# Decay stage: the products of q and k with their tables, on VectorE straight from PSUM

## The chip, the cores and the metric

One Trainium2 chip, one core of it. The kernel is one program on that core; the metric is the device time in microseconds (us), median of the runs shown. Engines are named as in the profile: PE (TensorE matrix products), PEld (its weight loads), DVE (VectorE), ACT (ScalarE), POOL (GpSimd), SP (SyncE).

## The reference, cut to what matters

Six blocks follow each other: two convolution blocks, an attention, a mixture of experts, a second attention ("L3", with a decay instead of a softmax) and a last mixture. The change lies in L3. For each of 16 images of 1024 tokens, taken as 4 sequences of 256 in blocks of 8 heads of 16 numbers:

```python
q = (x @ wq_w.T + wq_b).reshape(b, l, h, d)
k = (x @ wk_w.T + wk_b).reshape(b, l, h, d)
v = (x @ wv_w.T + wv_b).reshape(b, l, h, d)
phase = phazor_p / jnp.abs(phazor_p)
amp = jax.nn.sigmoid(amplitude)
phazor = phase * amp[:, None]
...
qc = q.astype(cplx) * (phazor_prog * phazor[None])[None]
cross = jnp.einsum('blhd,hde->blhe', qc, last_conv)
mask = jnp.where(tril[None], amp[:, None, None] ** jnp.where(tril, diff, 0)[None], 0.0)
qph = q.astype(cplx) * phase_prog[None]
kph = k.astype(cplx) * phase_prog_inv[None]
...
inner = jnp.einsum('bhlm,bmhd->blhd', qk_mask, v.astype(cplx))
out = (inner + cross).real.astype(x.dtype).reshape(b, l, h * d)
```

Each of q and k, bias added, is thus multiplied by tables over position and channel: k by one (`tab_k`), q by two (`tab_k` for the scores, `tab_s` for the state that comes from earlier chunks).

## The kernel before

The stages run one after the other; `decay_stage` (L2320) handles L3. It loops over 16 images (`images`, L2496: images -1, 0, 1, 14, 15, 16 written out, 2 to 13 in a loop). An image is 4 items (a = 0 to 3), an item being one half of the image's 1024 tokens (a // 2) and one group of 4 heads (a % 2); an item has 4 chunks of 128 tokens (c = 0 to 3). Item number w is 4 n + a. Every engine walks the same 16 places (a, c) of an image in an order written out by hand (`slots`, L2496 ff.), and they keep each other in step by counting semaphores. There is no scheduler.

At each place, in this order:

- PE (`body`, L3106): at c = 0 it projects the keys of the *next* item into `ps_q`, at c = 1 the queries of the next item (`project`, L3033); at c = 0 the scores of this item (`score`, L3051: 16 products of 32 rows into `ps_s`); in items 1 and 3 the keys and values in token order (`mix`, L3041); then transposes into `ps_x`, and `chunk` (L3063): the product with the state (`ps_o`), the new state (`ps_st`), and after c = 1 and c = 3 the inner products (L3093).
- DVE (`body`, L2877): at c = 0 `masked` for chunks 0 and 1 (scores times decay, `d_inner`, L2777), then one `masked` at each of c = 1 and c = 2; in items 1 and 3 `end_keys` (`d_k_tok`, `d_v_tok`, L2785); at c = 1 `add_item` (L2802); `new_state` (L2793), for which PE waits at the next chunk; in item 0 `combine` (L2865, L2867) and layer-norm statistics; in item 3 the gates.
- ACT (`body`, L2952): `copy_projection` (L2946) at c = 0 and 1, which adds the bias and writes `raw` in SBUF; the normalisations, the copies of `ps_x` and of `ps_o` (`d_o_chan`).
- POOL (`body`, L2625): in items 1 to 3, at each c, it waits until `masked` of this chunk is done and issues 1 or 2 of the 16 gathers of image n + 2 (`gather`, L2556, an indirect DMA of 128 rows; `GATHERS_AT`, L2447); at c = 0, behind them, `with_tables` (L2610): three products from `raw` with the tables. The gathers of c = 1 to 3 are queued behind these three.

`ps_q` is one buffer for both projections: PE's next `project` waits on `p_copied`, ACT's on `tables_used`.

Of the kernel before, what the change touches and what calls it, by code (L numbers as in the profile page):

```python
# [9 lines left out]
ALU = mybir.AluOpType  # L10
ACT = mybir.ActivationFunctionType
AX = mybir.AxisListType

P = 128
# [6 lines left out]
HALF = 512  # L21
# [2287 lines left out]
CHUNKS = 4  # L2309
# [10 lines left out]
def decay_stage(nc, T, route, slots_out, xT_dram, gates, ident, dram):  # L2320
    with ExitStack() as ctx:
        sb, ps, sem = allocator(nc, ctx)
# [12 lines left out]
        row = sb("d_row", [P, 2, 5])  # L2335
# [27 lines left out]
        tab_k = sb("d_tab_k", [P, 2, P])  # L2363
# [14 lines left out]
        shift = [sb(f"d_shift{k}", [P, TILES]) for k in range(2)]  # L2378
        xn = [sb(f"d_xn{k}", [P, PX]) for k in range(2)]
        xT = [sb(f"d_xT{k}", [P, PX]) for k in range(2)]  # L2380
        raw = sb("d_raw", [P, 2, HALF])
        q_chan = sb("d_q_chan", [P, 2, HALF])
        q_state = sb("d_q_state", [P, 2, HALF])
        k_chan = sb("d_k_chan", [P, 2, HALF])
# [39 lines left out]
        x_ready = sem("d_x_ready")  # L2424
        x_free = sem("d_x_free")
        p_ready = sem("d_p_ready")
        p_copied = sem("d_p_copied")
        tables_used = sem("d_tables_used")
        k_ready = sem("d_k_ready")
        k_done = sem("d_k_done")  # L2430
# [20 lines left out]
        def positive(eng, s, value):  # L2451
            if not (isinstance(value, int) and value <= 0):
                eng.wait_ge(s, value)
# [92 lines left out]
        def _(pool):  # L2546
# [60 lines left out]
                pool.wait_ge(rstd_done[k], 4 * m + 3)  # L2607
                nc.gpsimd.tensor_tensor(shift[k][:], zero[:], shift[k][:], ALU.subtract).then_inc(rstd_done[k], 1)  # L2608

            def with_tables(w, g, k):  # L2610

                pool.wait_ge(p_copied, 2 * w + 1)
                positive(pool, chunk_done, 4 * (w - 1))
                nc.gpsimd.tensor_tensor(
                    k_chan[:, k].rearrange("p (c l) -> p c l", c=CHUNKS),
                    raw[:, 0].rearrange("p (c l) -> p c l", c=CHUNKS),
                    tab_k[:, g:g + 1].broadcast_to([P, CHUNKS, P]), ALU.mult).then_inc(tables_used, 1)
                pool.wait_ge(p_copied, 2 * w + 2)
                for out, table in ((q_chan, tab_k), (q_state, tab_s)):
                    nc.gpsimd.tensor_tensor(  # L2620
                        out[:, k].rearrange("p (c l) -> p c l", c=CHUNKS),
                        raw[:, 1].rearrange("p (c l) -> p c l", c=CHUNKS),
                        table[:, g:g + 1].broadcast_to([P, CHUNKS, P]), ALU.mult).then_inc(tables_used, 1)

            def body(n):  # L2625
                finish, prepare, _ = parts_of(n)
                if isinstance(n, int) and n < 0:
                    scales(0, 0)
                for a, c, steps, nxt in slots(n):
                    if a and gathers(n):  # L2630
                        first = sum(some for at, some in GATHERS_AT.items() if at < (a, c))
                        if steps:
                            wait_apart(pool, inner_done, 4 * (4 * n + a) + c + 1, passed)
                        gather(n + 2, first, first + GATHERS_AT[a, c])
                    if (a, c) == (0, 3) and finish:
                        scales(n - 1, 1)
                    if (a, c) == (1, 3) and prepare and not (isinstance(n, int) and n < 0):
                        scales(n + 1, 0)
                    if c == 0 and nxt:
                        with_tables(4 * n + a + 1, (a + 1) % 2, (a + 1) % 2)  # L2640

            pool.wait_ge(step, TABLE_STEPS)
            images(pool, body)
# [2 lines left out]
        def _(dve):  # L2646
# [125 lines left out]
            def masked(w, c, g):  # L2772
# [4 lines left out]
                tt(inner[:, c].rearrange("p (j l) -> p j l", j=GH), ps_s[:, :, c * P:(c + 1) * P],  # L2777
                   decay[:, g * GH:(g + 1) * GH], ALU.mult).then_inc(inner_done, 1)

            def end_keys(n, half, c):  # L2780

                at = 8 * n + 4 * half + c
                dve.wait_ge(k_ready, at + 1)
                positive(dve, chunk_done, 4 * (4 * (n - 1) + 2 * half + 2))
                tt(k_tok[:, half, c], ps_k[:, 0:2 * P], tab_end[:].rearrange("p g r -> p (g r)"), ALU.mult)  # L2785
                nc.vector.tensor_copy(v_tok[:, half, c, :, 0:DH],
                                      ps_k[:, 2 * P:3 * P].rearrange("p (h e) -> p h e", h=HD)).then_inc(k_done, 1)
# [89 lines left out]
            def body(n):  # L2877
# [5 lines left out]
                    statistics(0, 0, 1)  # L2883
                for a, c, steps, nxt in slots(n):
                    w = 4 * n + a
                    if steps and c == 0:
                        masked(w, 0, a % 2)
                    if steps and c < CHUNKS - 1:
# [28 lines left out]
        def _(act):  # L2917
# [25 lines left out]
                    positive(act, xT_sent, 16 * (n - 1))  # L2943
                nc.scalar.activation(xT[k][:, half * HALF:half * HALF + HALF], ps_x[:], ACT.Copy).then_inc(x_free, 1)

            def copy_projection(w, g, kind):  # L2946
                act.wait_ge(p_ready, 2 * w + kind + 1)
                positive(act, tables_used, 3 * (w - 1) + (3 if kind else 1))
                nc.scalar.activation(raw[:, kind], ps_q[:], ACT.Identity, bias=row[:, g, 4 - kind:5 - kind]
                                     ).then_inc(p_copied, 1)  # L2950

            def body(n):  # L2952
                finish, prepare, _ = parts_of(n)
                first = isinstance(n, int) and n < 0
# [2 lines left out]
                    normalise(0, 0, 1)  # L2957
                for a, c, steps, nxt in slots(n):
                    w = 4 * n + a
                    if nxt and c < 2:  # L2960
                        copy_projection(w + 1, (a + 1) % 2, c)
                    for name in filled_at(n, a, c):
                        if name != "logits":
                            read_out(n, name)
# [15 lines left out]
        def _(pe):  # L2980
# [52 lines left out]
            def project(w, a, kind):  # L3033

                g, half = a % 2, a // 2
                positive(pe, p_copied, 2 * w + kind)
                weights = wq[:, g] if kind else wkv[:, g * P:(g + 1) * P]
                mm(ps_q[:], weights, xT[0][:, half * HALF:half * HALF + HALF], start=True, stop=True
                   ).then_inc(p_ready, 1)
# [166 lines left out]
```

## Time and profile before

| | |
|---|---|
| median of 3 runs | 4375.7 us (4369.7 to 4379.16) |
| the profiled execution | span 4435.5 us |
| decay stage in it | from about 2650 us to 3680 us; images 1 to 13 take 754 us |
| PE / DVE / ACT / POOL busy, whole span | 83% / 71% / 49% / 44% |

The page gives the busy time of each engine, the span in 40 slices, and the groups of instructions by line. The time of the profiled execution is known only by its span, and 59.8 us (1.4%) above the median of the runs that were not profiled. The queries used here are the windows (busy time of each engine in a stretch, with the granted TensorE clock), the groups by line, the waits, single lines, and the instructions in order of time.

### The profile page before, as it was taken

Reading aid. Unit: us, or ns where it says so; the run is one execution under the profiler, and the core shown is the slowest. Engines: PE = TensorE matmul, PEld = TensorE weight load, DVE = VectorE, ACT = ScalarE, POOL = GpSimd, SP = SyncE. Lnnn points to the kernel's source line nnn. Section 1 sums busy time; section 2 is a strip of 40 time slices with the busy share of each in tenths; the row PEclk is TensorE's granted clock in tenths of the full one; section 3 lists DMA queues with packets and bytes.
Section 4 is the critical chain, followed back from the end, with each engine's and each line's share of the span. In section 5 each row is a group of like instructions: output and inputs, shape, how many; then the busy total and the mean of one; then the engine's idle time right before and its main releaser. Section 6 shows DMA issues by size and latency. Waiting matters only on the chain. (4 is left out here: it accounts for less than half of the span.)

```text
span 4435.5 us, 74474 instructions
## 1 busy us (share of the span) xinstructions
PE 3699.2 (83%) x21807; PEld 1993.2 (45%) x21809; DVE 3136.1 (71%) x6481; ACT 2174.3 (49%) x3800; POOL 1933.4 (44%) x2119
## 2 busy tenths in 40 slices
PE   2479999999999999999569962888888886999999
PEld 0212333333333333332258851555555555777777
DVE  7478888888887878887156646555555557877777
ACT  3326666666666666666357740222222223444443
POOL 1111333233223333332345552666666644777776
PEclk9679999999999999999789985999999998999999
DMA  2121111122222222220033320000000001000000
GB/s 97 20 37 28 31 30 30 30 38 38 36 37 38 38 39 38 38 37 11 18 117 103 103 78 10 25 29 28 26 28 28 27 16 34 24 24 24 24 20 23
DMA packets 98451, 166.17 MB, mean 37 GB/s; under 512 B 27904, under 2 KB 33288, under 8 KB 98072
## 3 DMA queue, kind: packets, MB, share of 16 engines
q1 hardware_dynamic: 81208, 129.14, 12.2%
q0 software_dynamic: 16384, 33.59, 2.7%
q8 instruction: 134, 2.20, 0.2%
q14 instruction: 149, 1.22, 0.1%
q10 hardware_dynamic: 576, 0.02, 0.0%
HBM read 89.70 MB, written 72.97 MB: 37 GB/s over the span
## 5 line engine op out<-in xcount | busy, mean ns | idle before, releaser
L1214 ACT ACTIVATE b_probs<-b_ps_s 128x512 f32<-128x512 f32 x2048 | 1174.4, 596 | 673.0 <-PE b_ps_s L1258 609.9
L1016 DVE TENSOR_REDUCE b_maxes<-b_ps_m 128x1 f32<-128x1024 f32 x1024 | 1218.2, 1216 | 312.9 <-PE b_ps_m L1246 288.4
L1258 PE MATMUL b_ps_s<-b_qs,b_ks 99*128 99x512 bf16 x2048 | 790.6, 390 | 83.8 <-DMA b_qs<-b_m_parts 23.4
L1246 PE MATMUL b_ps_m<-b_ks,b_qs 96*128 96x512 bf16 x2048 | 638.5, 394 | 64.2 <-DVE b_maxes L1016 43.5
L1985 POOL TENSOR_TENSOR e_act_lo<-e_act,e_act_hi 128x512 fp32r<-128x512 f32 x384 | 522.6, 1361 | 238.9 <-DVE e_act_hi L1914 238.9
L1258 PEld LDWEIGHTS b_ps_s<-b_qs,b_ks 99*128 99x128 bf16 x2048 | 198.7, 98 | 882.5 <-ACT b_probs L1214 668.2
L1270 PE MATMUL b_ps_o<-b_probs,b_vs 128*32 128x512 f32 x4096 | 551.8, 611 | 23.6 <-ACT b_probs L1214 22.8
L2186 ACT ACTIVATE e_act<-e_ps_h,e_bias 128x512 f32<-128x512 f32 x384 | 264.4, 689 | 411.3 <-PE e_ps_h L2240 290.6
L935 POOL DMA_INDIRECT slots_in<-b_xn,b_slot x256 | 251.6, 983 | 413.2 <-ACT b_probs L1214 367.0
L2089 DVE TENSOR_TENSOR e_act<-e_act,e_ps_g 128x512 f32<-128x512 f32 x384 | 261.6, 682 | 145.7 <-ACT e_act L2186 145.7
L2777 DVE TENSOR_TENSOR d_inner<-d_ps_s,d_decay 128x512 f32<-128x512 f32 x256 | 169.3, 682 | 221.6 <-PE d_ps_s L3059 109.3
L2556 POOL DMA_INDIRECT d_y<-slots_out,d_slot_now x256 | 248.5, 971 | 121.1 <-issue 59.0
L1246 PEld LDWEIGHTS b_ps_m<-b_ks,b_qs 96*128 96x128 bf16 x2048 | 193.0, 100 | 236.8 <-DVE b_maxes L1016 107.3
L1914 DVE CAST e_act_hi<-e_act 128x512 fp32r<-128x512 f32 x384 | 244.6, 637 | 0.0
L2238 PE MATMUL e_ps_h<-e_x_hi,e_w_hi 128*128 128x512 f32 x384 | 159.0, 414 | 47.8 <-DVE e_x_lo L2073 42.5
L2971 ACT ACTIVATE d_o_chan<-d_ps_o 128x512 f32<-128x512 f32 x64 | 38.2, 597 | 322.4 <-PE d_ps_o L3093 283.3
L1577 DVE SCALAR_TENSOR_TENSOR c_act<-c_ps_h,c_bias,c_half_way 128x512 f32<-128x512 f32 x142 | 106.5, 750 | 101.5 <-ACT c_half_way L1658 98.9
L2934 ACT ACTIVATE d_xn<-tokens,d_shift,d_rstd 128x128 f32 (+1 forms) x256 | 104.9, 482 | 138.4 <-POOL d_shift L2608 138.4
L1270 PEld LDWEIGHTS b_ps_o<-b_probs,b_vs 128*32 128x32 f32 x4096 | 81.2, 108 | 197.3 <-issue 143.3
L897 POOL TENSOR_TENSOR b_taken<-b_hit 128x64 bf16<-128x64 f32 x16 | 5.2, 323 | 361.0 <-DVE b_hit L1077 361.0
L2250 PE MATMUL e_ps_y<-e_act_hi,e_w_hi 128*128 128x512 f32 x384 | 152.4, 397 | 1.1 <-POOL e_act_lo L1985 1.1
L2239 PE MATMUL e_ps_h<-e_x_lo,e_w_hi 128*128 128x512 f32 x384 | 153.1, 399 | 0.0
(462 smaller groups left out, 7089.7 us busy)
## 6 DMA issues: line engine op xcount, KB each, us to landing
b_qs<-b_q_parts SPq DMA_DIRECT2D x96, 256.0 KB
c_xin<-slots_in SPq DMA_DIRECT2D x71, 256.0 KB, 2.6
slots_out<-c_y_out SPq DMA_DIRECT2D x71, 256.0 KB, 2.0
b_q_parts<-b_qparts SPq DMA_DIRECT2D x16, 768.0 KB
a_x<-in_x_dram SPq DMA_DIRECT2D x8, 1024.0 KB, 10.2
normalised_t<-d_xT SPq DMA_DIRECT2D x16, 512.0 KB
e_xb<-normalised_t SPq DMA_DIRECT2D x32, 256.0 KB, 2.8
out_dram<-e_total SPq DMA_DIRECT2D x32, 256.0 KB, 2.0
```

Source lines behind the costliest of these rows:

```text
L935: nc.gpsimd.indirect_dma_start(out=slots_in, out_offset=bass.IndirectOffsetOnAxis(ap=slot[:, i:i + 1], axis=0), in_=xn[1][:, j * P:(j + 1) ...
L1016: nc.vector.tensor_reduce(maxes[:, kv, u:u + 1], ps_m[:, u % 2], AX.X, ALU.max).then_inc(m_free, 1)
L1214: nc.scalar.activation(probs[:, s % PROBS, j * HALF:(j + 1) * HALF], ps_s[:, j % 2], ACT.Exp).then_inc(exp_done, 1)
L1246: last = nc.tensor.matmul(ps_m[:, u % 2, half * HALF:(half + 1) * HALF], qs[0:STACK, buffer, h * PX + qt * P:h * PX + qt * P + P], ks[0:ST ...
L1258: nc.tensor.matmul(ps_s[:, j % 2], ks[0:rows, parity, kv * PX + tt * P:kv * PX + tt * P + P], qs[0:rows, parity, h * PX + half * HALF:h * ...
L1270: last = nc.tensor.matmul(ps_o[32 * j:32 * j + 32, :], vs[:, parity, tt, g // 2, :], probs[:, s % PROBS, j * HALF:(j + 1) * HALF], start=( ...
L1914: copy(act_hi[:, u % ring_a], act_buf[:, u % RING]).then_inc(hi_done, 1)
L1985: nc.gpsimd.tensor_tensor(act_lo[:, u % ring_a], act_buf[:, u % RING], act_hi[:, u % ring_a], ALU.subtract).then_inc(lo_done, 1)
L2089: nc.vector.tensor_tensor(act_buf[:, u % RING], act_buf[:, u % RING], ps_g[:, (u // units_of_gate) % 2], ALU.mult).then_inc(weighed, 1)
L2186: nc.scalar.activation(act_buf[:, u % RING], ps_h[:, u % ring_h, 0], ACT.Gelu, bias=bias[:, bias_column(u, 0)]).then_inc(a_ready, 1)
L2556: nc.gpsimd.indirect_dma_start(out=y[:, i // TILES, i % TILES], out_offset=None, in_=slots_out, in_offset=bass.IndirectOffsetOnAxis(ap=slo ...
L2777: tt(inner[:, c].rearrange("p (j l) -> p j l", j=GH), ps_s[:, :, c * P:(c + 1) * P], decay[:, g * GH:(g + 1) * GH], ALU.mult).then_inc(inn ...
```

## The change

VectorE computes (ps_q + bias) * table in one `scalar_tensor_tensor` from PSUM, three times an item, each into the same tile as before. ACT's copy, POOL's three products, the tile `raw` and the semaphore `p_copied` are gone. PE's `project` now waits for VectorE's reads of `ps_q` (`tables_used`).

```diff
@@ POOL
-            def with_tables(w, g, k):
-                pool.wait_ge(p_copied, 2 * w + 1)
-                positive(pool, chunk_done, 4 * (w - 1))
-                nc.gpsimd.tensor_tensor(k_chan[:, k]..., raw[:, 0]...,
-                    tab_k[:, g:g + 1].broadcast_to([P, CHUNKS, P]), ALU.mult).then_inc(tables_used, 1)
-                pool.wait_ge(p_copied, 2 * w + 2)
-                for out, table in ((q_chan, tab_k), (q_state, tab_s)):
-                    nc.gpsimd.tensor_tensor(out[:, k]..., raw[:, 1]..., table..., ALU.mult).then_inc(tables_used, 1)
...
-                    if c == 0 and nxt:
-                        with_tables(4 * n + a + 1, (a + 1) % 2, (a + 1) % 2)
@@ DVE
+            def keys_with_table(w, g):
+                dve.wait_ge(p_ready, 2 * w + 1)
+                positive(dve, chunk_done, 4 * (w - 1))
+                stt(laid(k_chan[:, g]), laid(ps_q[:]), row[:, g, 4:5], tab_k[:, g:g + 1].broadcast_to([P, CHUNKS, P]),
+                    ALU.add, ALU.mult).then_inc(tables_used, 1)
+
+            def queries_with_tables(w, g):
+                dve.wait_ge(p_ready, 2 * w + 2)
+                for out, table in ((q_chan, tab_k), (q_state, tab_s)):
+                    stt(laid(out[:, g]), laid(ps_q[:]), row[:, g, 3:4], table[:, g:g + 1].broadcast_to([P, CHUNKS, P]),
+                        ALU.add, ALU.mult).then_inc(tables_used, 1)
...
                 for a, c, steps, nxt in slots(n):
                     w = 4 * n + a
+                    if nxt and c == 0:
+                        keys_with_table(w + 1, (a + 1) % 2)
+                    if nxt and c == 1:
+                        queries_with_tables(w + 1, (a + 1) % 2)
                     if steps and c == 0:
                         masked(w, 0, a % 2)
@@ ACT
-                    if nxt and c < 2:
-                        copy_projection(w + 1, (a + 1) % 2, c)
@@ PE, project
-                positive(pe, p_copied, 2 * w + kind)
+                positive(pe, tables_used, 3 * w + kind)
```

PE's order is the same in both. DVE's order in item 3 (shown of image 14, which is written out), from the start of the item to the keys in token order of chunk 1 (`d_k_tok`, for which PE waits), before (L2777 is `masked`, L2785 `end_keys`, L2793 `new_state`, L2809 to L2819 the gates):

```order
L2777 TENSOR_TENSOR d_inner<-d_ps_s,d_decay 128x512 x2
L2785 TENSOR_TENSOR d_k_tok<-d_ps_k,d_tab_end 128x256
L2786 COPY d_v_tok<-d_ps_k 128x8x16
L2793 TENSOR_TENSOR d_state<-d_ps_k,d_block_mask 128x128
L2809 TENSOR_TENSOR d_logits<-d_ps_x,d_bg 128x64
L2816 MAX d_top<-d_logits 128x8 x8
L2819 TENSOR_TENSOR d_gap<-d_top 128x8
L2777 TENSOR_TENSOR d_inner<-d_ps_s,d_decay 128x512
L2785 TENSOR_TENSOR d_k_tok<-d_ps_k,d_tab_end 128x256
```

and in the change (its lines are numbered anew: L2768 and L2775 are the new products, L2758 `masked`, L2783 `end_keys`, L2791 `new_state`):

```order
L2768 SCALAR_TENSOR_TENSOR d_k_chan<-d_ps_q,d_row,d_tab_k 128x512
L2758 TENSOR_TENSOR d_inner<-d_ps_s,d_decay 128x512 x2
L2783 TENSOR_TENSOR d_k_tok<-d_ps_k,d_tab_end 128x256
L2784 COPY d_v_tok<-d_ps_k 128x8x16
L2791 TENSOR_TENSOR d_state<-d_ps_k,d_block_mask 128x128
L2807 TENSOR_TENSOR d_logits<-d_ps_x,d_bg 128x64
L2814 MAX d_top<-d_logits 128x8 x8
L2817 TENSOR_TENSOR d_gap<-d_top 128x8
L2775 SCALAR_TENSOR_TENSOR d_q_chan<-d_ps_q,d_row,d_tab_k 128x512
L2775 SCALAR_TENSOR_TENSOR d_q_state<-d_ps_q,d_row,d_tab_s 128x512
L2758 TENSOR_TENSOR d_inner<-d_ps_s,d_decay 128x512
L2783 TENSOR_TENSOR d_k_tok<-d_ps_k,d_tab_end 128x256
```

One product now stands ahead of the first `masked`, and two ahead of that of chunk 2 and of everything of chunk 1 behind it.

POOL's order from item 1 into item 2 of an image (image 1, written out; L2556 is one gather), before:

```order
L2556 DMA d_y<-slots_out,d_slot_now 128x128
L2614 TENSOR_TENSOR d_k_chan<-d_raw,d_tab_k 128x512
L2620 TENSOR_TENSOR d_q_chan<-d_raw,d_tab_k 128x512
L2620 TENSOR_TENSOR d_q_state<-d_raw,d_tab_s 128x512
L2556 DMA d_y<-slots_out,d_slot_now 128x128 x5
```

and in the change, the same place in the loop (REGISTER_ALU computes the value of a wait; L2554 is one gather):

```order
L2554 DMA d_y<-slots_out,d_slot_now 128x128
L63 REGISTER_ALU
L2554 DMA d_y<-slots_out,d_slot_now 128x128
L63 REGISTER_ALU
L2554 DMA d_y<-slots_out,d_slot_now 128x128 x2
L63 REGISTER_ALU
L2554 DMA d_y<-slots_out,d_slot_now 128x128
```

The three products between the gathers are gone; each gather now stands behind its own wait (for `masked` of its chunk) alone.

## Rows read from the trace of the kernel before

**Rows 1.** Windows: length, busy time (count) by engine, granted clock, DMA share.
```profile
core 0: us, PE busy (x) PEld busy (x) DVE busy (x) ACT busy (x) POOL busy (x), PEclk, DMA share, GB/s
2794.85:3548.56 753.71, 617.54 (x5604) 414.34 (x5600) 421.88 (x1694) 212.53 (x428) 463.66 (x495) 0.92 0.09 27
3201.82:3220.02 18.20, 15.06 (x125) 9.83 (x121) 9.26 (x51) 2.18 (x4) 11.62 (x12) 0.91 0.10 29
3247.26:3257.81 10.55, 9.13 (x104) 6.40 (x101) 3.69 (x8) 6.02 (x13) 9.18 (x11) 1.00 0.20 68
3569.30:3580.48 11.18, 8.88 (x101) 5.89 (x97) 8.02 (x23) 1.97 (x3) 3.86 (x3) 0.92 0.01 2
3580.48:3596.70 16.22, 12.99 (x121) 8.63 (x117) 11.42 (x52) 6.24 (x13) 8.28 (x11) 1.00 0.01 4
3596.70:3605.38 8.68, 8.51 (x105) 6.07 (x101) 3.69 (x8) 6.24 (x13) 3.80 (x3) 1.00 0.15 58
3605.38:3620.25 14.87, 12.98 (x124) 9.01 (x121) 9.20 (x51) 2.07 (x4) 3.77 (x3) 1.00 0.01 2
...
3220.02:3230.92 10.90, 8.49 (x101) 5.93 (x97) 8.75 (x28) 1.86 (x3) 3.89 (x3) 0.95 0.02 6
3230.92:3247.26 16.34, 14.12 (x120) 8.91 (x116) 11.08 (x50) 6.24 (x13) 10.93 (x14) 0.93 0.06 16
```

**Rows 2.** Waits of PE and DVE in 2700:3560: total us, times, longest.
```profile
PE d_ps_k L3084 <- DVE d_v_tok L2786: 53.0, 51, 4.4
...
DVE d_inner L2777 <- remote: 109.0, 15, 8.1
```

**Rows 3.** Groups by line, 3000:3600: shapes, count, busy us, mean ns, idle before.
```profile
L2777 DVE TENSOR_TENSOR d_inner<-d_ps_s,d_decay 128x512 f32<-128x512 f32 x166 | 109.7, 682 | 147.6 <-remote 79.7 <-PE d_ps_s L3059 67.9
...
L2614 POOL TENSOR_TENSOR d_k_chan<-d_raw,d_tab_k 128x512 f32<-128x512 f32 x42 | 53.8, 1281 | 47.9 <-ACT d_raw L2949 47.1
```

**Rows 4.** Single lines: duration in ns as minimum/median/maximum.
```profile
L1577 DVE SCALAR_TENSOR_TENSOR c_act<-c_ps_h,c_bias,c_half_way x142: 735/751/752, 2260.0 to 2620.4; 128x512 f32<-128x512 f32 x142
...
L2865 DVE SCALAR_TENSOR_TENSOR d_y<-d_y,d_weight_now,tokens x128: 337/344/2327, 2725.1 to 3577.8; 128x128 f32<-128x128 f32 x128
```

**Rows 5.** In time, item 0: start, duration, operation, idle before and releaser.
```profile
3225.99 2.14 DVE L2865 SCALAR_TENSOR_TENSOR d_y<-d_y,d_weight_now,tokens 128x128 f32<-128x128 f32 x4
3226.09 1.38 POOL L2620 TENSOR_TENSOR d_q_state<-d_raw,d_tab_s 128x512 f32<-128x512 f32 x1
...
3228.99 0.49 PE L3077 MATMUL d_ps_o<-d_q_state,d_state 128*128 128x128 f32 x2 [1.92 <-DVE d_state L2793]
```

**Rows 6.** In order of time, chunk 1 of item 3, image 14.
```profile
3613.80 0.46 PE L3084 MATMUL d_ps_k<-d_state,d_turn 128*128 128x128 f32 x2 [0.40 <-DVE d_v_tok L2786]
```

**Rows 7.** In order of time, chunk 1 of item 2 in a late image.
```profile
3600.69 0.69 ACT L2949 ACTIVATE d_raw<-d_ps_q,d_row 128x512 f32<-128x512 f32 x1 [0.61 <-PE d_ps_q L3038]
...
3601.12 0.42 DVE L2802 TENSOR_TENSOR tokens<-tokens,d_ps_x 128x256 f32<-128x256 f32 x1
...
3602.26 0.66 PE L3027 MATMUL d_ps_x<-ident,d_xn 128*128 128x128 f32 x4
```

**Rows 8.** In time, start of item 3: image with gathers, then one without.
```profile
3204.79 0.95 POOL L2556 DMA_INDIRECT d_y<-slots_out,d_slot_now  x1 [0.30 <-issue]
...
3206.94 1.29 DVE L2777 TENSOR_TENSOR d_inner<-d_ps_s,d_decay 128x512 f32<-128x512 f32 x2 [8.05 <-remote]
...
3208.81 0.49 PE L3084 MATMUL d_ps_k<-d_state,d_turn 128*128 128x128 f32 x2 [1.40 <-DVE d_v_tok L2786]
...
3607.67 1.29 DVE L2777 TENSOR_TENSOR d_inner<-d_ps_s,d_decay 128x512 f32<-128x512 f32 x2 [3.75 <-PE d_ps_s L3059]
...
3610.45 0.39 PE L3084 MATMUL d_ps_k<-d_state,d_turn 128*128 128x128 f32 x2
```

**Rows 9.** In order of time, item 0 of the first image.
```profile
2758.20 0.95 POOL L2556 DMA_INDIRECT d_y<-slots_out,d_slot_now  x1 [0.30 <-issue]
...
2760.70 3.11 DVE L2865 SCALAR_TENSOR_TENSOR d_y<-d_y,d_weight_now,tokens 128x128 f32<-128x128 f32 x4 [4.90 <-DMA d_y<-slots_out,d_slot_now]
```

More of the change, by code:

```diff
@@ L2380, in decay_stage @@
         xT = [sb(f"d_xT{k}", [P, PX]) for k in range(2)]
-        raw = sb("d_raw", [P, 2, HALF])
         q_chan = sb("d_q_chan", [P, 2, HALF])
@@ L2426, in decay_stage @@
         p_ready = sem("d_p_ready")
-        p_copied = sem("d_p_copied")
         tables_used = sem("d_tables_used")
@@ L2608, in scales @@
                 nc.gpsimd.tensor_tensor(shift[k][:], zero[:], shift[k][:], ALU.subtract).then_inc(rstd_done[k], 1)
-            def with_tables(w, g, k):
-                pool.wait_ge(p_copied, 2 * w + 1)
-                positive(pool, chunk_done, 4 * (w - 1))
-                nc.gpsimd.tensor_tensor(
-                    k_chan[:, k].rearrange("p (c l) -> p c l", c=CHUNKS),
-                    raw[:, 0].rearrange("p (c l) -> p c l", c=CHUNKS),
-                    tab_k[:, g:g + 1].broadcast_to([P, CHUNKS, P]), ALU.mult).then_inc(tables_used, 1)
-                pool.wait_ge(p_copied, 2 * w + 2)
-                for out, table in ((q_chan, tab_k), (q_state, tab_s)):
[L2620 to L2623, printed above, removed]
             def body(n):
@@ L2778, in masked, with laid @@
                    decay[:, g * GH:(g + 1) * GH], ALU.mult).then_inc(inner_done, 1)
+            def laid(x):
+                return x.rearrange("p (c l) -> p c l", c=CHUNKS)
+            def keys_with_table(w, g):
[8 more added lines that the diff above has]
+                        ALU.add, ALU.mult).then_inc(tables_used, 1)
             def end_keys(n, half, c):
@@ L2944, in read_out @@
                 nc.scalar.activation(xT[k][:, half * HALF:half * HALF + HALF], ps_x[:], ACT.Copy).then_inc(x_free, 1)
[L2946 to L2950, printed above, removed]
             def body(n):
```

## The prediction, made before the changed kernel ran

> **What bounds the kernel now.** I read the windows by item first. An item runs from one key projection on PE to the next; images 1 to 13 take 753.71 us, 57.98 each, with PE busy 617.54 of it and a mean granted clock of 0.92 [rows 1]. Image 14 is the same program without gathers and shows what the bare chain takes: items 0 to 3 in 11.18, 16.22, 8.68 and 14.87 us, 50.95 together [rows 1]. Against that stand, in an image with gathers, 10.90, 16.34, 10.55 and 18.20 [rows 1]. So items 0 and 1 are as short as they can be, item 2 loses 1.9, and item 3 loses 3.3 in this image. The shown image takes 55.99; the mean one loses 7.03 (57.98 − 50.95).
>
> Then the waits: DVE stands in front of `masked` at the start of item 3 fifteen times, 109.0 us in all, and the profile names no engine for it ("remote") [rows 2]; PE waits 53.0 us in 51 places for the tokens' keys of DVE (`d_v_tok`) [rows 2]. In order of time at item 3: the item starts at 3201.82 [rows 1]; POOL's last gather runs from 3204.79 for 0.95 us; DVE's `masked`, which waits for PE's score products, starts at 3206.94 after 8.05 us idle, 5.12 after the item's start; PE's chunk product stands until 3208.81, 1.40 of it for DVE [rows 8]. In the image without gathers the same `masked` starts 2.29 after the item's start (3607.67 − 3605.38) and the chunk product 5.07 after (3610.45 − 3605.38), not 6.99 [rows 1, 8]. The hold is thus 2.8 us on DVE and about 1.9 to 2.0 on PE, and it ends 1.2 us after the last gather's end. I read it so: the completion of PE's narrow score products is seen late while POOL's gathers are in flight. Why these gathers lie there: POOL works in order, and the gathers of places 1 to 3 are queued behind three table products of 1281 ns each [rows 3], which wait for both projections. They come out in a burst at the end of the item and fall on the scores of the next one.
>
> So in this stage PE and DVE hand work to each other, and PE is late where DVE is late; POOL and ACT are not the bound but POOL decides when gathers go.
>
> **The change part by part.** Every time below is for one image (4 items) unless said.
>
> *Removed from ACT:* eight copies of PSUM, 0.69 us each [rows 7], with ACT busy 2.2 of 18.2 us in item 3 and 6.0 of 10.6 in item 2 [rows 1]. No wait of PE rests on them; in item 2 ACT's other copies feed PE and move 0.7 earlier, but DVE is later there (below). Worth 0.
>
> *Removed from POOL:* twelve products of 1.28, 15.4 us of the 35.7 it is busy (463.66 / 13) [rows 1, 3]. By itself nothing waits for that; it moves the gathers, priced below.
>
> *Added to DVE:* twelve `scalar_tensor_tensor` of 128x512, one input in PSUM. The nearest row is the same operation on the same shape out of PSUM with a second tensor in SBUF, 735 to 752 ns, median 751 [rows 4]; the lower bound is the product without the bias, 682 [rows 3]. I take 0.75: 9.0 us an image, on a DVE that is busy 32.5 of 58 (421.88 / 13) [rows 1]. What of it lies on the path:
>
> - Item 0. At its start DVE has the key product extra, while its first `masked` waits for PE anyway; 0.7 of idle covers it. The two query products (1.5) come at chunk 1, ahead of `masked` and `new_state`, for which PE already waits 1.92 us [rows 5]. No cover: +1.4 with 0.1 of overlap. Against it stands a gain. DVE's four combine steps took 2.14 us there while a POOL product ran beside them for 1.38 [rows 5]; their usual length is 0.337, their longest 2.327 [rows 4]. Four undisturbed take 1.35, and with no POOL product beside them they give back the 2.14 − 1.35 = 0.8, and 1.0 where one takes 1.36. I take 1.0. Sum +0.4.
> - Item 1. The same 1.4 at chunk 1, and at chunk 0 DVE is still at the statistics of the layer norm when the keys come, (it is busy 11.08 of 16.34 there [rows 1]), so that I estimate half of a key product (0.4) to delay `masked`. +1.8.
> - Item 2. PE does not wait for DVE in chunk 1, but DVE's addition to `tokens` (3601.12, 0.42 long) must precede PE's transposes at 3602.26: slack 0.7 [rows 7]. The queries are there at 3600.69, when ACT takes them [rows 7], and with 1.5 of products ahead of `masked` and of the addition, the addition moves by up to 1.6. 1.6 − 0.7 = +0.9.
> - Item 3. At chunk 1 PE waits 0.40 for `d_v_tok` [rows 6], so the queries' 1.4 goes through. At chunk 0 DVE idles 3.75 us even without gathers [rows 8], which hides the key product. +1.4.
>
> Together +4.5 on DVE's part of the chain; with 0.682 for a product +3.9; and with nothing covered 9.0 − 1.0 = +8.0.
>
> *Gained by moved gathers.* The change puts each gather behind its own `masked` alone. They then spread over the item, and no burst should fall on the next scores: item 2 gets back 10.55 − 8.68 = 1.9, item 3 its 2.0 [rows 1, 8]. −3.9, between −3.9 and 0. In the first image a combine takes 3.11 us after 4.90 of waiting for a gather's data; its gather ran at 2758.20 [rows 9]. There the next images' gathers come about 3.7 us (three products) earlier. −4 once.
>
> *The rest of the loss.* 7.03 − 3.9 = 3.1 us an image is neither bare chain nor hold. The granted clock is 0.91, 0.95, 0.93 and 1.00 in items 3, 0, 1 and 2 with gathers, and 0.92, 1.00, 1.00, 1.00 without [rows 1]; the two levels are 2.4 and 1.2 GHz, and the low one follows PE's idle time, that in front of `d_v_tok` in item 3 foremost. With the holds gone, that idle time (1.40) is gone, but PE idles 1.4 longer at each chunk 1. It lies between 0 (as in image 14) and 3.1 (as now). I take 1.1, nearer the row without holds.
>
> An image is then 50.95 + 4.5 + 1.1 = 56.5, against 57.98: −1.5, and −19.5 for thirteen. Image 14 has no hold to lose: +4.5, and +1.0 for some low clock, +5.5. The last has no next projection after its third item: +3. The first: −4. Sum −15. The profiled execution, 4435.5, would be 4420.5. Its 59.8 above the median is a length of the whole program under the profiler and I leave it in place: 4375.7 − 15 = **4361**.
>
> *New waits.* PE's next `project` waits for DVE's last read of `ps_q`. That read comes within 3 us of the projection and the next one is over 5 us off: nothing. DVE waits for `p_ready` with `masked`, `d_k_tok` and `new_state` queued behind. PE projects first in each place, so this wait is for one product, 0.6 to 0.7 us, and is in the terms above.
>
> **The rivals.**
>
> *A. The holds stay* (slower). The gathers still run on POOL, still 16 an image; if the late completion comes from something else at the start of items 2 and 3, or the spread gathers hit other narrow products (the inner ones after chunks 1 and 3), then nothing of the 3.9 comes back. It decides as soon as less than 2.5 us an image is regained with the clock as forecast (4.5 − 2.0), less than 4.5 with the clock as now. At nothing regained an image is 50.95 + 4.5 + 3.9 + 3.1 = 62.5: 13 × 4.5 = +58, then +5.5, +3 and −4 for image 14, the last and the first: 4438. For it: the profile gives no releaser for DVE's wait ("remote"), only coincidence in time. Against it: the 2.29 and 5.12 us of [rows 8], and items 0 and 1, over which no burst falls and which are not longer than in image 14 [rows 1]. A page bears on this rival, and by it the time would be that of A. The Trainium skill, page "SBUF — State Buffer", section "SBUF: two separate sides", says that engines' and DMAs' ports do not contend and that only VectorE and GpSimd share a pair, while PE never waits for anyone; by that rule gathers could not hold PE's products. The same section has that a shared pair is locked for a whole instruction; by that rule, the combine of [rows 5] stands still for POOL's product, and the trace agrees (2.14 for 1.35). Chance 0.2.
>
> *B. The holds go, but the clock loss stays as now,* 3.1 an image in place of 1.1, since PE idles 1.4 longer four times. 13 × (−1.5 + 2.0) = +6.5, image 14 +7, the ends −1: +12, 4388. For it: the clock fell in items 0, 1 and 3, behind idle times of 1 to 2 us. Against it: image 14 ran at 1.00 through items 1 to 3 with waits of 0.4 for DVE [rows 1, 6]. Chance 0.25, of which a third ends within 0.2%.
>
> *C. More is gained:* clock as in image 14, a product at 0.68: 13 × (−1.5 − 1.1 − 0.6) = −42, image 14 +4, the ends −1: −39, and with half of the 0.6 −35: some 4338. Chance 0.1.
>
> *D. The scores come no earlier for DVE but the burst only moves* into items 0 or 1, with half of the hold left. +25 against the forecast: 4386, the same as B. It is in B's chance.
>
> **How the numbers follow.** The forecast (0.45) is 4361 with 4345 to 4377 from its own terms (half a microsecond an image on the clock, as much on the DVE terms). A 0.2, B with D 0.25, C 0.1. A measurement of this kernel tells about 0.2%, 8.7 us, from no change. Faster: most of the forecast (0.36) and C (0.10), 0.46. Within 0.2%: 0.09 of the forecast, 0.08 of B, 0.04 of A where part is regained: 0.21. Slower: 0.16 of A, 0.17 of B: 0.33. The range 4335 to 4420 holds the forecast, C nearly whole and B; out of it stay A with nothing regained, and little below.
>
> **What would show each step.** The new products read 0.68 to 0.75 each. DVE's "remote" wait ahead of `masked` in item 3 is gone, and `masked` starts 2.3 us after the item; if it still starts 5 us after, A. The windows give item 2 at about 9.6, item 3 at 16.3 to 17; item 0 at 11.5 and item 1 at 18. The longest step of L2865 (now L2863) falls from 2.3 to under 1 us. PE's waits for `d_v_tok` and `d_state` at chunk 1 grow by 1.4 each; a growth of more than 2 makes the DVE terms too small. The clock of images 1 to 13 rises above 0.95 for the forecast, stays at 0.92 for B. In image 14, which has no gathers, the DVE terms stand alone: 50.95 should become 55.5 to 56.5.

## The result, and the profile after

The change makes the kernel slower: 4399.16 us (4394.34 to 4401.94, 4 runs) against 4374.86 (4369.7 to 4379.16, 4 runs), a ratio of 1.0056 with a 95% interval of 1.0042 to 1.0071. That is +24 us where −15 was forecast: inside the stated range, on the other side of zero, in the place of rival B (4388). But it did not come about as B said.

The first thing to see is a contradiction. The profiled execution of the changed kernel has a span of 4397.3 us, 2 below its own time; that of before, on which every term of the prediction rests, 4435.5, 60 above the times of before. By the two profiles the change gains 38 us, by the timed runs it loses 24. So the kernel before was profiled once more (first run below). From here on "before" is that second execution, span 4366.7, and where the first is meant the text says so.

Windows of before (second execution): twelve images from one start of item 3 to another (2842.05 to 3485.89), then items 3, 0, 1 and 2 of one image. Columns as in [rows 1]:

```profile
core 0: us, PE busy (x) PEld busy (x) DVE busy (x) ACT busy (x) POOL busy (x), PEclk, DMA share, GB/s
2842.05:3485.89 643.84, 536.42 (x5189) 364.95 (x5185) 389.58 (x1596) 197.76 (x396) 426.79 (x457) 0.96 0.10 29
3379.28:3394.05 14.77, 13.04 (x124) 9.02 (x120) 9.14 (x51) 2.13 (x4) 11.26 (x12) 1.00 0.12 31
3394.05:3404.51 10.46, 8.06 (x101) 5.71 (x97) 8.18 (x24) 1.97 (x3) 4.65 (x4) 0.99 0.04 13
3404.51:3421.33 16.82, 14.60 (x120) 9.40 (x117) 11.51 (x52) 6.24 (x13) 10.97 (x14) 0.90 0.05 16
3421.33:3431.87 10.54, 8.67 (x104) 6.07 (x100) 3.69 (x8) 6.12 (x13) 9.18 (x11) 0.99 0.21 68
```

The same of the changed kernel, the twelve images and one image with gathers:

```profile
2844.82:3507.75 662.93, 536.77 (x5189) 365.64 (x5185) 472.94 (x1740) 135.15 (x300) 243.11 (x313) 0.96 0.09 29
3118.91:3134.99 16.08, 13.04 (x124) 9.02 (x120) 11.20 (x54) 0.81 (x2) 5.01 (x6) 1.00 0.09 25
3134.99:3146.86 11.87, 9.17 (x101) 6.54 (x97) 10.36 (x32) 0.60 (x1) 0.00 (x0) 0.89 0.00 0
3146.86:3163.74 16.88, 13.45 (x121) 8.82 (x117) 12.16 (x50) 4.98 (x11) 10.70 (x16) 0.98 0.08 23
3163.74:3173.66 9.92, 8.60 (x105) 6.08 (x101) 5.66 (x11) 4.86 (x11) 4.52 (x5) 1.00 0.22 79
```

An image of before takes 53.65 us (643.84 / 12), not the 57.98 of [rows 1]; one of the changed kernel 55.24. PE's own work is the same to 0.1% (536.42 and 536.77) at the same clock, so what was added is waiting. DVE works 83 us more, 7 an image; POOL 184 less, ACT 63 less. Item 3, which in [rows 1] took 18.20, takes 14.77 in the image shown, no more than in the image without gathers (14.87). Over the twelve images it averages 15.4 (184.68 / 12): seven times 14.8 to 14.9, five times 15.8 to 16.5 with a granted clock of 0.89 to 0.93. Item 2 loses most, 10.54 here and 11.1 on average (133.07 / 12) against 8.68; the changed kernel has 9.92 there, and 9.93 on average.

The last image but one has no gathers, so none has a part in how the two kernels differ there. Its items 0 to 3 in the changed kernel, to hold against the rows from 3569.30 on in [rows 1]:

```profile
3523.83:3535.31 11.48, 8.88 (x100) 6.25 (x97) 10.07 (x31) 0.60 (x1) 0.00 (x0) 0.91 0.01 1
3535.31:3552.60 17.29, 13.70 (x120) 8.83 (x117) 12.50 (x51) 4.97 (x11) 4.52 (x8) 0.96 0.01 3
3552.60:3562.11 9.51, 8.55 (x104) 6.07 (x100) 5.66 (x11) 4.86 (x11) 0.00 (x0) 1.00 0.13 52
3562.11:3578.30 16.19, 12.98 (x124) 9.02 (x120) 11.25 (x54) 0.81 (x2) 0.00 (x0) 1.00 0.01 2
```

Single lines of the changed kernel, the answers to [rows 3] and [rows 4] (duration in ns as minimum/median/maximum): the three new products and the combine.

```profile
L2768 DVE SCALAR_TENSOR_TENSOR d_k_chan<-d_ps_q,d_row,d_tab_k x64: 717/750/753, 2741.7 to 3604.5; 128x512 f32<-128x512 f32 x64
...
L2775 DVE SCALAR_TENSOR_TENSOR d_q_chan<-d_ps_q,d_row,d_tab_k x64: 731/750/752, 2745.0 to 3607.4; 128x512 f32<-128x512 f32 x64
L2775 DVE SCALAR_TENSOR_TENSOR d_q_state<-d_ps_q,d_row,d_tab_s x64: 739/742/748, 2745.7 to 3608.0; 128x512 f32<-128x512 f32 x64
...
L2863 DVE SCALAR_TENSOR_TENSOR d_y<-d_y,d_weight_now,tokens x128: 337/343/353, 2724.5 to 3531.8; 128x128 f32<-128x128 f32 x128
```

The products cost what the nearest row said, and no combine step is stretched any more.

### The profile page after: what moved, and what is told of

It is laid out like the page before. It is cut to its first block and busy times, and to the rows that moved or that the text cites. A ratio compares the mean times of both kernels' runs of the same rounds, so it can differ in the third digit from the quotient of the medians.

```text
span 4397.3 us, 74090 instructions
## 1 busy us (share of the span) xinstructions
PE 3660.1 (83%) x21809; PEld 1973.2 (45%) x21809; DVE 3241.9 (74%) x6673; ACT 2091.6 (48%) x3672; POOL 1685.1 (38%) x1927
## 5 line engine op out<-in xcount | busy, mean ns | idle before, releaser
L2554 POOL DMA_INDIRECT d_y<-slots_out,d_slot_now x256 | 245.1, 957 | 261.6 <-DVE d_inner L2758 181.6
L2758 DVE TENSOR_TENSOR d_inner<-d_ps_s,d_decay 128x512 f32<-128x512 f32 x256 | 169.2, 682 | 20.9 <-PE d_ps_s L3053 20.9
L2230 PE MATMUL e_ps_g<-e_g_rows,e_spread 128*128 128x512 f32 x384 | 150.9, 393 | 2.3 <-DVE e_act L2089 2.3
```

Of the source, the lines that this page charges most:

```text
L2554: nc.gpsimd.indirect_dma_start(out=y[:, i // TILES, i % TILES], out_offset=None, in_=slots_out, in_offset=bass.IndirectOffsetOnAxis(ap=slo ...
```

## The experiments

### The kernel before, profiled again

No edit.

> The kernel before once more, to see how its profiled execution stands to its timed runs. Theory 1: the late products at the start of items 2 and 3 (PE's scores seen late while gathers run) belong to that one profiled execution and not to the runs that were timed; a second profile then has a span near 4374 us, images of 53 to 54.5 us in the middle, and DVE's waits for 'remote' in item 3 are few. Theory 2: they come with every profile of this kernel and not in timed runs: span again 4430 to 4440, images of 58. Theory 3: they are in the timed runs too, and the 60 us are elsewhere: span between the two, images of 58. Ratio 1.000 in all.

Measured: 4370.24 us against 4371.46 for the copies of before beside it (ratio 0.9997, 0.9986 to 1.0009), profiled span 4366.7. Of 34 timed runs of before in these experiments none was above 4384.7. Theory 1 holds: the images take 53.65 us, and no wait of DVE is put down to "remote". The start of an item 3 in this execution, in order of time (start, duration, operation, idle before and what ended it), to hold against [rows 8]:

```profile
3378.86 1.00 POOL L2556 DMA_INDIRECT d_y<-slots_out,d_slot_now  x1 [0.16 <-issue]
...
3380.17 0.95 POOL L2556 DMA_INDIRECT d_y<-slots_out,d_slot_now  x1 [0.30 <-issue]
3380.34 0.98 PEld L3059 LDWEIGHTS d_ps_s<-d_q_chan,d_k_chan 32*128 32x128 f32 x32 [0.76 <-issue]
3380.34 1.17 PE L3059 MATMUL d_ps_s<-d_q_chan,d_k_chan 32*128 32x128 f32 x32
...
3381.42 0.95 POOL L2556 DMA_INDIRECT d_y<-slots_out,d_slot_now  x1 [0.30 <-issue]
...
3381.68 1.29 DVE L2777 TENSOR_TENSOR d_inner<-d_ps_s,d_decay 128x512 f32<-128x512 f32 x2 [4.45 <-PE d_ps_s L3059]
```

Gathers run before, beside and after the scores, as in the first execution, and yet `masked` starts 0.17 us after the scores end (3380.34 + 1.17), with PE and not "remote" as releaser. That is 2.40 after the item's start at 3379.28, as without gathers (2.29). The first execution has the hold in fourteen items 3, with 2.5 to 3.7 us from the end of the scores to `masked` (and once in an item 2); in the same fourteen items of this one it is 0.18 us at most. The hold belonged to one of the two executions, and gathers beside the scores do not by themselves bring it about.

### The scales moved ahead on POOL

The kernel before, with one move:

```diff
                 for a, c, steps, nxt in slots(n):
+                    if (a, c) == (1, 2) and prepare and not (isinstance(n, int) and n < 0):
+                        scales(n + 1, 0)
                     if a and gathers(n):
...
-                    if (a, c) == (1, 3) and prepare and not (isinstance(n, int) and n < 0):
-                        scales(n + 1, 0)
```

> The kernel before with one move on POOL: the four small steps that make the layer-norm scales of the next image (d_rstd, d_shift) stand ahead of the gathers of item 1, chunk 2, in place of behind those of chunk 3. Theory 1 (before's item 2 takes 10.5 to 11.2 us and not 8.7 because POOL comes to these steps some 5.6 us after DVE's d_mv, its queue being filled by table products and gathers, and ACT's xn and PE's transposes wait for them): item 2 falls to 8.7 to 9.3, 1 to 2 us an image: 4345 to 4358. Theory 2 (it is the gathers themselves that hold item 2): same as before within 4 us, 4367 to 4375.

Measured: 4349.88 against 4373.2 (ratio 0.9945, 0.9925 to 0.9965), 23 us faster. Theory 1. Item 2 falls to 8.90, in eleven of twelve images, with table products and gathers all still on POOL (item 3 gives 0.6 of it back on average, so that an image takes 52.26 for 53.65):

```profile
3350.57:3359.47 8.90, 8.52 (x104) 6.06 (x100) 3.69 (x8) 6.20 (x13) 7.48 (x8) 1.00 0.26 88
```

What held item 2 is thus a chain over POOL that the prediction had not seen. In before, in order of time, from DVE's means over POOL's scales and ACT's normalisation to PE's transposes (the second set, in the item 2 that starts at 3421.33 and takes 10.54):

```profile
3415.36 0.64 DVE L2769 BATCH_NORM_AGGREGATE d_mv<-d_stats 128x2 f32<-128x6 f32 x8
...
3422.85 0.22 POOL L2602 TENSOR_TENSOR d_rstd<-d_mv,d_eps 128x8 f32<-128x8 f32 x1
...
3425.51 1.65 ACT L2934 ACTIVATE d_xn<-tokens,d_shift,d_rstd 128x128 f32 x4 [2.24 <-POOL d_shift L2608]
...
3427.63 1.64 ACT L2934 ACTIVATE d_xn<-tokens,d_shift,d_rstd 128x128 f32 x4
...
3429.88 0.65 PE L3027 MATMUL d_ps_x<-ident,d_xn 128*128 128x128 f32 x4 [1.34 <-ACT d_xT L2944]
```

The means are there at 3416.00; POOL, with two table products and four gathers still ahead, begins the scales 6.85 later. Item 2 grows with this delay: in the twelve images of before it is 5.6 to 8.7 us late, and item 2 takes 9.27 at the one end and 13.55 at the other. In `scales_early` and in the changed kernel the same two steps:

```profile
3344.60 0.64 DVE L2769 BATCH_NORM_AGGREGATE d_mv<-d_stats 128x2 f32<-128x6 f32 x8
...
3347.14 0.21 POOL L2602 TENSOR_TENSOR d_rstd<-d_mv,d_eps 128x8 f32<-128x8 f32 x1
```

```profile
3157.77 0.64 DVE L2750 BATCH_NORM_AGGREGATE d_mv<-d_stats 128x2 f32<-128x6 f32 x8
...
3160.75 0.21 POOL L2600 TENSOR_TENSOR d_rstd<-d_mv,d_eps 128x8 f32<-128x8 f32 x1
```

1.90 and 2.34 us: this is the relief that the change brings, and a move of one call brings it without loading DVE.

### Only the keys, only the queries

`keys_only` leaves `keys_with_table` on DVE and gives the queries back to ACT's copy and two POOL products; `queries_only` is the other half. Each has a semaphore of its own for keys and queries in place of `tables_used`.

```diff
 (keys_only)
                     if nxt and c == 0:
                         keys_with_table(w + 1, (a + 1) % 2)
-                    if nxt and c == 1:
-                        queries_with_tables(w + 1, (a + 1) % 2)
```

> Only the key product on DVE, straight from PSUM, at chunk 0; the queries go over ACT's copy and two POOL products as before (one POOL product fewer in front of the gathers). Theory: the key product hides under DVE's wait for the scores except in item 1: 4374 to 4382. Rival (the cost lies in the key product ahead of masked at chunk 0): 4390 or more.

> Only the two query products on DVE at chunk 1; the keys go over ACT's copy and one POOL product as before. Theory: this part carries nearly the whole of the loss: 4390 to 4400. Rival (keys carry it): 4370 to 4380.

Measured: keys only 4346.11 (ratio 0.9955, 0.9938 to 0.9972), 25 us faster than before; queries only 4395.77 (1.0056, 1.0037 to 1.0076), 24 slower. Over the twelve images:

```profile
2836.01:3460.51 624.50, 531.84 (x5188) 363.17 (x5184) 425.70 (x1644) 165.05 (x348) 366.43 (x408) 0.96 0.10 30
```

```profile
2844.60:3502.10 657.50, 527.14 (x5188) 361.88 (x5184) 438.28 (x1692) 167.95 (x348) 306.67 (x361) 0.97 0.10 29
```

52.04 and 54.79 an image. The queries carry the whole loss, as expected. The keys were expected to cost 3 to 10 us and gave 25: the key product hides under DVE's wait for the scores, and one POOL product fewer in front of the scales is a gain that no theory had named before the run. The two halves do not add up (−25 and +24 give +24 together): the relief of POOL pays once, and `queries_only` has already taken it (its item 2 averages 9.93 us, as in the full change).

> keys_only with the same move of the scales on POOL. Theory 1: keys_only took its gain (25 us) from the shorter POOL queue ahead of the scales, item 2 at 9.3; what is left there is 0.3 to 0.6 us an image: 4336 to 4346. Theory 2 (its gain comes from elsewhere): gains add up, 4325 to 4332.

Measured: 4340.83 (0.9925, 0.9902 to 0.9947). Theory 1, with its number: moving the scales gives 23 us alone and 5 to 7 on top of `keys_only` (by the medians, and by each against its own copies of before). It is in the main one and the same gain.

### One more product at chunk 1

```diff
-                for out, table in ((q_chan, tab_k), (q_state, tab_s)):
+                for out, table in ((q_chan, tab_k), (spare, tab_s), (q_state, tab_s)):
```

> The change with one more product of the queries on DVE at chunk 1 (a spare 128x512 product from PSUM into a tile that nobody reads, between the two). It prices DVE's time at that place. Theory 1 (DVE's products at chunk 1 lie on the path in items 0, 1 and 3 nearly whole, in item 2 nearly whole too): 0.75 us each, 2 to 3 us an image, 32 to 48 over the change: 4430 to 4447. Theory 2 (they are mostly covered, and the change's loss is clock or a wait of PE): below 4410.

Measured: 4447.29 (ratio to before 1.0160, 1.0137 to 1.0184), 48 over the change, the upper end of theory 1, with an image at 58.65 (703.80 / 12). The products are 64 times 0.742 = 47 us, so DVE's time at chunk 1 seems to count in full. Not all of it is waiting, though: over the twelve images (40.9 us longer, 48 products more) PE's busy time for the same matmuls grows by 15.3, from 536.77 to 552.02, at a clock of 0.93 for 0.96. That leaves 25.6 us of waiting, 0.53 for a product of 0.742; the low clock makes up the rest.

### Where DVE's products stand

Placements of the same two query products. `q_behind_state`: after `new_state` of chunk 1; `q_split`: one ahead of chunk 1, one ahead of chunk 2; `q_at_c2`: both at the end of chunk 2; `mix`: keys on DVE, queries on DVE behind `new_state` in item 2 only, else on POOL.

```diff
 (q_behind_state)
-                    if nxt and c == 1:
-                        queries_with_tables(w + 1, (a + 1) % 2)
...
                     if steps and state_index(0, a, c) is not None:
                         new_state(n, a, c)
+                    if nxt and c == 1:
+                        queries_with_tables(w + 1, (a + 1) % 2)
```

> The change with the two query products moved behind new_state in chunk 1, everything else as in the change. Theory: the cost of the change is DVE's 1.4 us ahead of masked, the tokens' keys and new_state in chunk 1, of which PE waits; with the products behind them nearly all of 1.5 us an image (24 us) comes back: 4365 to 4380. Rival (the cost comes from the moved gathers or from PE's new wait on DVE's reads of ps_q): stays within 5 us of the change, 4394 to 4404.

Measured: 4434.39 (1.0149, 1.0132 to 1.0166), 35 slower than the change: a clear miss, and neither theory had it. Item 2 did fall to 8.9. In item 3, which starts at 3130.12 here and at 3118.91 in the changed kernel, the wait moved from chunk 1 to chunk 2. The changed kernel:

```profile
3128.58 0.49 PE L3078 MATMUL d_ps_k<-d_state,d_turn 128*128 128x128 f32 x2 [1.65 <-DVE d_v_tok L2784]
...
3132.10 0.49 PE L3078 MATMUL d_ps_k<-d_state,d_turn 128*128 128x128 f32 x2 [1.01 <-DVE d_v_tok L2784]
...
3133.20 0.91 PE L3042 MATMUL d_ps_k<-d_wkv,d_xT 128*128 128x384 f32 x2 [0.38 <-DVE d_state L2791]
```

and `q_behind_state`:

```profile
3138.45 0.49 PE L3078 MATMUL d_ps_k<-d_state,d_turn 128*128 128x128 f32 x2 [0.32 <-DVE d_v_tok L2784]
...
3143.29 0.80 PE L3078 MATMUL d_ps_k<-d_state,d_turn 128*128 128x128 f32 x2 [2.32 <-DVE d_v_tok L2784]
...
3144.90 1.65 PE L3042 MATMUL d_ps_k<-d_wkv,d_xT 128*128 128x384 f32 x2 [0.38 <-DVE d_state L2791]
```

Both wait 2.65 us in two pieces and reach the product of chunk 2 equally late (13.19 and 13.17 after the item's start). But after the single wait of 2.32 the same PE work takes 1.65 in place of 0.91: the clock has gone to its low level, and the item ends at 18.12, not 16.08. Nine of the twelve items 3 of `q_behind_state` take 18.1 us. So do two of the twelve of the changed kernel, and there the clock fell behind the wait of 1.65:

```profile
3228.39:3246.52 18.13, 15.70 (x124) 10.52 (x120) 11.36 (x54) 0.81 (x2) 5.01 (x6) 0.81 0.08 22
```

One long wait thus goes with the low clock far more often than two shorter ones, but it is neither needed for it nor proven to be its cause. What the low clock costs, PE's busy time over the twelve images of `q_behind_state` shows:

```profile
2846.27:3536.28 690.01, 560.95 (x5188) 379.84 (x5184) 474.62 (x1740) 135.15 (x300) 242.74 (x312) 0.92 0.09 28
```

2.02 us an image more than in the changed kernel for the same matmuls (560.95 − 536.77, by 12), of the 2.26 that an image is longer (57.50 − 55.24).

> The change with its two query products apart: q_chan at the start of chunk 1, q_state at the start of chunk 2. In q_behind_state both fell on one wait of PE (2.3 us at chunk 2) where the change has two waits of 1.7 and 1.1; the waits summed to the same and yet an image took 2.3 us longer, with PE's own work slower (granted clock 0.91 for 0.95). Theory 1 (the price is DVE's time on the path, plus clock where one wait grows long): waits of 1.0 and 1.8 in the odd items, as the change but for item 2, where one product less stands ahead of the addition to tokens (-0.7): 4385 to 4398. Theory 2 (only the sum of DVE's products at these places counts): 4394 to 4404.

Measured: 4422.67 (1.0115, 1.0092 to 1.0137); a miss for both. An item 1 with the low clock and one without, of the same program:

```profile
3158.84:3179.42 20.58, 16.26 (x120) 10.25 (x117) 13.55 (x55) 4.98 (x11) 10.70 (x16) 0.83 0.11 32
3273.69:3291.70 18.01, 13.07 (x120) 8.62 (x116) 13.30 (x55) 4.98 (x11) 10.71 (x16) 1.00 0.09 22
```

2.57 us apart, and in both PE waits 2.32 at chunk 0 and 1.47 at chunk 2; the items ahead of them are alike too (10.71 us each at a clock of 1.00). In the long one and in the short one, the wait at chunk 0 and the next product of the tokens' keys:

```profile
3164.62 0.49 PE L3078 MATMUL d_ps_k<-d_start,d_turn 128*128 128x128 f32 x2 [2.32 <-DVE d_v_tok L2784]
3166.83 1.49 PE L3042 MATMUL d_ps_k<-d_wkv,d_xT 128*128 128x384 f32 x2
...
3279.47 0.49 PE L3078 MATMUL d_ps_k<-d_start,d_turn 128*128 128x128 f32 x2 [2.32 <-DVE d_v_tok L2784]
3280.88 0.81 PE L3042 MATMUL d_ps_k<-d_wkv,d_xT 128*128 128x384 f32 x2
```

So `q_state`, moved into chunk 2, pushes DVE's work of item 0 into item 1, and a wait of 2.32 appears where the change has 0.8 in ten of its twelve images. The clock fell after it in one image and not in the other, so the wait does not settle it. Nine of the twelve images have an item 1 of over 20 us.

> The change with both query products at the end of DVE's chunk 2. In item 3 PE takes no new state at chunk 3 and so waits for no token keys there; item 1 still does. Theory 1 (what counts is who waits behind the products): item 3 at 15 to 16 us, item 2 at 8.9, item 1 as in the change, 17.4; 4365 to 4385. Theory 2 (any place costs the 1.5 us): 4394 or more.

Measured: 4362.67 (0.9976, 0.9962 to 0.9989), 12 faster than before and 36 faster than the change, with the same products on the same engine. Theory 1. PE now waits elsewhere too, at 28 starts of items, for the reads of `ps_q` (waits from 2700 to 3530: total us, times, longest):

```profile
PE d_ps_k L3078 <- DVE d_v_tok L2784: 52.4, 61, 1.9
...
PE d_ps_q L3032 <- DVE d_q_state L2775: 34.0, 28, 1.6
...
PE d_ps_o L3071 <- DVE d_state L2791: 23.1, 30, 3.6
```

where the changed kernel has:

```profile
PE d_ps_k L3078 <- DVE d_v_tok L2784: 79.0, 72, 2.3
...
PE d_ps_o L3071 <- DVE d_state L2791: 40.2, 28, 4.8
```

119.2 us became 109.5; the single buffer of the projections takes 34.0 of what the place gives back. Gone as well are 11.5 us that PE of the changed kernel waits in item 2 for `tokens`, behind the products. By items the theory's numbers came out: item 3 takes 15.7 us on average, item 2 8.95 and item 1 17.4. An image takes 53.16 (637.88 / 12) against 55.24, at the same clock of 0.96.

> keys_only with the two query products of one item in four on DVE as well: those made in item 2, behind new_state of chunk 1 (q_behind_state had item 2 at 8.9 us with them there). Theory 1: no cost on DVE there, POOL has two products fewer in item 2 and its gathers come earlier: 4338 to 4347. Theory 2 (queries on DVE cost in any item): 13 times 1 to 1.5, 4360 or more.

> mix with the scales moved ahead on POOL, as in keys_scales. mix and keys_scales already have item 2 at 8.9 us in most images. Theory 1: nothing adds up: 4336 to 4346. Theory 2: 4335 or less.

Measured: 4344.89 (0.9927, 0.9902 to 0.9951) and 4339.98 (0.9928, 0.9905 to 0.9951). Theory 1 both times. With `keys_scales` they are the best versions here, 28 to 36 us faster than before by their medians and 54 to 59 faster than the change; between them there is no difference that could be told. In all three the keys are on DVE. Queries on DVE cost nothing that could be told in item 2, where PE takes no tokens' keys.

### The copy kept on ACT

The change, but DVE multiplies from ACT's copy in SBUF (bias already added):

```diff
-                dve.wait_ge(p_ready, 2 * w + 2)
+                dve.wait_ge(p_copied, 2 * w + 2)
                 for out, table in ((q_chan, tab_k), (q_state, tab_s)):
-                    stt(laid(out[:, g]), laid(ps_q[:]), row[:, g, 3:4], table[:, g:g + 1]..., ALU.add, ALU.mult)
+                    tt(laid(out[:, g]), laid(raw[:, 1]), table[:, g:g + 1]..., ALU.mult)
```

> The change with ACT's copy (bias added) kept: DVE multiplies from the copy in SBUF, not from PSUM. Theory 1 (the one pass from PSUM saves ACT's 0.69 us of latency ahead of DVE's products): DVE's products start 0.5 to 0.9 later at chunk 1, 2 to 3 us an image: 4420 to 4445. Theory 2 (DVE is busy until then anyway): 4395 to 4405.

Measured: 4460.03 (1.0214, 1.0182 to 1.0246), beyond theory 1. The products are a little shorter from SBUF, but they stand behind ACT:

```profile
L2776 DVE TENSOR_TENSOR d_q_chan<-d_raw,d_tab_k 128x512 f32<-128x512 f32 x34 | 23.5, 690 | 22.2 <-ACT d_raw L2951 22.2
```

```profile
3154.29 0.49 PE L3086 MATMUL d_ps_k<-d_state,d_turn 128*128 128x128 f32 x2 [2.52 <-DVE d_v_tok L2784]
```

PE's wait in chunk 1 of item 3 is 2.52 where the change has 1.65. Here too the low clock adds to the wait: over the twelve images PE is busy 556.81 us for 536.77, at 0.93 for 0.96, 20 of the 43 us that they are longer. Clock included, the one pass from PSUM is worth 61 us against this form. If the products are on DVE at this place at all, it is the right way to make them.

## Why the prediction was wrong, point by point

- **What bounds the kernel.** PE and DVE in turns: right. The loss of 7.03 us an image was not the kernel's but one execution's. In before as it is timed 53.65 − 50.95 = 2.7 are lost, 2.4 of it in item 2.
- **The step that failed** is the one in the last sentence of the sum: "Its 59.8 above the median is a length of the whole program under the profiler and I leave it in place." The stage itself was 54 us longer in that execution (twelve images at 58.17 by 698.06 / 12, by the windows of the same kind, against 53.65), so the difference sat in the rows I was pricing, and nearly all of it in one of them: item 3 averages 19.8 in that execution (237.98 / 12) and 15.4 in the other. Three terms were read off it: the hold of item 3 (−2.0), most of the clock (−2.0), and the base of 57.98 from which they were subtracted. What the runs showed in its place: before at 53.65 an image, no hold in item 3, no clock to win. The changed kernel's own image was not far off, 56.5 forecast and 55.24 measured (here [rows 1] gave the bare chain); what it was compared with was 4.3 too long. The trace gave a warning that I named and passed over: fifteen waits of DVE with no releaser known to the profile ("remote") [rows 2]. Fourteen of them lie in items 3 and one in an item 2, not all in item 3 as the prediction has it.
- **The base of rival A.** Chance 0.2 stood on the holds staying. What happened is neither: before as timed had none in item 3 to lose. By that second execution, the sentence beside rival A on the Trainium skill, page "SBUF — State Buffer", section "SBUF: two separate sides" (engines and DMAs do not contend, PE waits for no one), has the trace on its side: scores beside gathers are done 0.17 us before `masked` begins. The late starts of the first execution stay unexplained and decide nothing about it. The other half of the rule, the pair shared by VectorE and GpSimd, is also borne out: with POOL's products gone the longest combine step fell from 2.327 us (2.207 in the second execution) to 0.353.
- **DVE's terms were right.** In the image without gathers they stand alone (measured from [rows 1]; against the second execution the sum is +3.7):

| item | forecast | measured |
|---|---|---|
| 0 | +0.4 | 11.48 − 11.18 = +0.3 |
| 1 | +1.8 | 17.29 − 16.22 = +1.1 |
| 2 | +0.9 | 9.51 − 8.68 = +0.8 |
| 3 | +1.4 | 16.19 − 14.87 = +1.3 |
| sum | +4.5 | +3.5 |

  Only item 1 was sized too large. What the terms left out is that more waiting can also bring more of the low clock (`q_twice`, `q_behind_state`); in the change as it is, that sum came out at nothing.
- **The gain in item 2: right size, wrong cause.** 1.9 was forecast and was to be had (`scales_early`: 8.90). I put it down to gathers that fall on the scores. It is POOL's lateness with `d_rstd`, which ACT and PE wait for; the four small steps that make the scales stand in no sentence of the prediction. The change regains it (from 11.1 on average to 9.9, with 0.8 to 0.9 of it its own DVE term), and that is why an image costs +1.6 and not +3.5. That the size fitted is luck.
- **The clock.** 1.1 for 3.1 was forecast. Before and after are both at 0.96: no term at all. (The prediction also gives the clocks of the image without gathers in a wrong order: the 0.92 is that of its item 0, item 3 has 1.00 [rows 1]. No sum rests on it.)
- **Put together,** in the prediction's own terms for an image: +4.5 for DVE, −1.9 for item 2, −2.0 for item 3 and −2.0 of clock were forecast, −1.4 (−1.5 as rounded there); +3.5, −1.9, 0 and 0 came, +1.6. Twelve images at +1.59 make 19.1 us, and from there to the last key projection the changed kernel takes 7.2 more (95.63 against 88.46), 3.5 to 3.7 of it in the image without gathers. The two profiled spans differ by 30.6 us (4397.3 − 4366.7), the medians of the timed runs by 24. Rival B gave 4388, 11 us from the measured time, by a loss of clock that did not occur: that it lay nearest is luck, and so is the place of 4399 in the stated range.

What stays open: what held DVE's `masked` in that one execution. That a completion of PE was seen late is a reading, no row names it. It did not come again, so nothing here could be tried on it. Open is also what decides whether the clock falls behind a given wait.

## What to carry to other kernels

Before a trace is priced, set its span beside the timed runs; where they differ by more than their spread, find the stage where the difference sits, and take no term from that stage's rows until a second execution has shown them. Taking work off an idle-looking engine can pay through something small at the end of its queue, so follow what each of its last items releases: here moving four tiny operations ahead gave as much as moving a third of the products to another engine. And on the engine that hands work to PE, the place of an operation decides more than its length: the same three products made the kernel 63 us slower than before, 24 slower, or 12 faster.

## What the runs showed of the hardware

- The granted clock fell behind waits of PE of 1.65 and 2.32 us, but not each time. In item 3 of the changed kernel, after waits of 1.65 and 1.01, a group of 128x384 products took 0.91 us; in `q_behind_state`, after one wait of 2.32, it took 1.65, and the item 2.0 us longer. Yet two of twelve items 3 of the changed kernel fell to 0.81 behind the wait of 1.65, and of two items of `q_split` that both wait 2.32, with like items ahead of them, one ran at 0.83 and one at 1.00.
- DVE's operation behind PE's narrow score products, with indirect DMAs beside them, started 2.5 to 3.7 us after their end in fourteen items of one execution, with no releaser known, and 0.07 to 0.18 us after it in the next. One execution out of those profiled had this.
- A combine step of DVE (two inputs in SBUF, 0.34 us) took up to 2.2 and 2.3 us in the two executions of before, where POOL multiplies in SBUF, and 0.353 at most in the changed kernel, where it does not.
- The same product of 128x512 took 750 ns from PSUM with the bias added and 690 from SBUF without.
